# Second products of four experts with tokens as the moving side, their bias in ScalarE's copy and a turn back on TensorE; the last stage's ranks and shares rebuilt; edge codes spread over another loop

## The reference, cut to what matters

```
# first stage: out = prelu(((d_gamma * (q k^T)) v) Wo + bo)      q, k, v = x W + b, 1024 tokens, batch 4
# last stage, on y = layernorm(h):
hg = (y @ W_gat).reshape(M, 4, 4)                    # heads x experts
a_src, a_dst = (hg * att_src).sum(-1), (hg * att_dst).sum(-1)
e = leaky_relu(a_src[src] + a_dst[dst])              # 262144 edges and the loops
alpha = softmax of e over the edges of each dst
agg = segment_sum(hg[src] * alpha, dst) + b_gat
scores = layernorm(agg, ln_gamma, ln_beta).reshape(M, 4, 4).mean(1)
w = softmax(top_k(scores, 2))
for ei in range(4):
    hh = gelu(y @ W1[ei] + b1[ei])
    out = out + g[..., None] * (hh @ W2[ei] + b2[ei])   # g: w where ei is among the two, else 0
```

## Time and profile before

| | us |
|---|---|
| median of 3 runs | 1418.79 (1412.3 to 1440.24) |
| the profiled execution's own time | 1412.49 |
| its span in the trace | 1410.0 |

### The profile page before, as it was taken

One profiled execution on the slowest core, in us unless ns is written; L12 is line 12 of the kernel. 1 busy time (PEld: TensorE's weight loads), 2 busy tenths in 40 slices (PEclk: granted clock), 3 DMA queues, 4 the chain that ended last, 5 costly groups with the idle time before them and its releaser, 6 DMA issues. The chain is left out here.

```text
span 1410.0 us, 29905 instructions
## 1 busy us (share of the span) xinstructions
PE 1122.6 (80%) x11867; PEld 648.3 (46%) x11867; DVE 985.3 (70%) x2120; ACT 460.0 (33%) x855; POOL 277.9 (20%) x312
## 2 busy tenths in 40 slices
PE   2499279999999999999938999995956989588440
PEld 1232144556555565555626333333425767577340
DVE  3645547898888889898355355554464994799977
ACT  1120144355534344343325344443111233322120
POOL 0000450010010101001003000000000577777505
PEclk9799689999999999999955899997975696799785
DMA  6000220000000000000010443402020211011001
GB/s 217 0 8 16 81 91 2 3 2 3 2 3 13 7 2 3 3 2 7 10 57 6 106 90 82 87 5 49 20 66 0 17 10 10 9 10 9 0 1 31
DMA packets 54835, 40.15 MB, mean 28 GB/s; under 512 B 27171, under 2 KB 51363, under 8 KB 53684
## 3 DMA queue, kind: packets, MB, share of 16 engines
q1 hardware_dynamic: 49588, 36.70, 10.3%
q0 software_dynamic: 5120, 1.65, 1.6%
HBM read 14.80 MB, written 4.94 MB: 14 GB/s over the span
## 5 line engine op out<-in xcount | busy, mean ns | idle before, releaser
L1100 DVE CUSTOM_DVE_ANT_0 ps<-ps,arena 128x512 f32<-128x512 f32 (+3 forms) x384 | 209.0, 595 | 60.1 <-PE ps L878 59.1
L1046 ACT ACTIVATE arena<-ps 128x512 f32<-128x512 f32 (+1 forms) x320 | 160.0, 552 | 211.3 <-PE ps L903 211.2
L892 PE MATMUL ps<-arena 32*128 32x256 f32 (+3 forms) x1856 | 213.9, 350 | 3.1 <-ACT arena L1046 2.3
L878 PE MATMUL ps<-arena 32*128 32x512 f32 (+3 forms) x768 | 167.4, 531 | 9.9 <-DVE arena L1100 9.4
L892 PEld LDWEIGHTS ps<-arena 32*128 32x128 f32 (+1 forms) x1856 | 138.1, 183 | 73.3 <-issue 49.7
L1865 POOL DMA_INDIRECT arena<-node_table,arena x160 | 151.9, 949 | 55.5 <-issue 48.4
L1450 DVE TENSOR_SCALAR arena<-ps 128x704 bf16<-128x704 f32 x96 | 85.6, 892 | 78.1 <-PE ps L1393 78.1
L817 POOL TENSOR_SCALAR_AFFINE_SELECT arena<-arena 128x512 f32<-128x512 f32 (+1 forms) x72 | 41.5, 597 | 459.9 <-ACT arena L1046 413.2
L925 PE MATMUL ps<-arena 128*32 128x256 f32 (+3 forms) x1856 | 110.3, 322 | 0.9 <-POOL arena L817 0.3
L929 PE MATMUL ps<-arena 128*32 128x256 f32 (+3 forms) x1856 | 106.3, 312 | 0.0
L1430 ACT ACTIVATE arena<-ps 128x704 bf16<-128x704 f32 x96 | 72.2, 757 | 97.1 <-PE ps L1393 97.1
(11 more groups left out here) (299 smaller groups left out, 1848.8 us busy)
## 6 DMA issues: line engine op xcount, KB each, us to landing
arena<-arena SPq DMA_DIRECT2D x144, 88.0 KB, 2.2
arena<-in_L_tok_d_gamma_batched SPq DMA_DIRECT2D x4, 1024.0 KB, 13.6
arena<-node_table,arena POOLq DMA_INDIRECT x160, 2.4
arena<-xT SPq DMA_DIRECT2D x8, 264.0 KB, 4.1
xT<-in_L_ffn_edge_index SPq DMA_DIRECT2D x2, 1024.0 KB, 7.6
dT<-arena SPq DMA_DIRECT2D x12, 88.0 KB, 2.1
arena<-in_x SPq DMA_DIRECT2D x4, 256.0 KB, 9.4
dT<-arena SPq DMA_DIRECT2D x8, 128.0 KB, 2.3
```

The lines of the kernel that those rows point to most:

```text
L878: last = pe.matmul(to[:, hd % 2, at:at + wd], qu[r, P * j:P * j + P], ku[r, lo:lo + wd], start=(at == 0), stop=True, skip_group_check=True)
L892: pe.matmul(to[0:r, hd % 2, at:at + wd], ku[d, P * j:P * j + r], qu[d, lo:lo + wd], start=(at == 0), stop=False, skip_group_check=True)
L1046: last = act.activation(to[:, x, 0:at + wd], src[:, x, 0:at + wd], ACT.Exp, scale=unit)
L1100: last = dve.tensor_tensor_reduce(tile, tile, distance[:, first:first + wd], 1.0, most if lo > 0 else -3e38, ALU.add, ALU.max, most)
```

## The change

1. **Edge codes.** The 16 instructions become 32 on half the columns. They are issued between VectorE's products with gamma, from the third step (g = 2) up to g = 26 of the 32, by `while g >= 2 and edges < min(32, 32*(g-1)//25)`. `shi` and `dhi` lie in `keys` and `tmp` now. The loads of the edge list are issued after those of gamma and of the second pair.
2. **The row of ones** is set once, by GpSimd, in the second norm; VectorE's two memsets go.
3. **Features** use 64 rows of `xT` and `wg`, so nothing waits for a zeroed row; the expert products wait until the features are copied out of PSUM banks 0 and 1.
4. **Second products**: `W2` of an expert is stationary (64 wide), the 384 tokens of hidden values move; two experts fill the two halves of a PSUM bank. ScalarE copies that bank with the bias `b2` as a per-partition operand, TensorE turns the result back with 3 transposes, and ScalarE copies the turned chunk as before. There are four hidden tiles instead of two, and the second half of a chunk is worked off in the next one, so that there are 12 rounds for 11 chunks. GpSimd's addition of `b2` goes.
5. **Last stage**: no scaling of the mean and of the average (folded into other constants), gamma's product placed behind the variance, rank constants set by GpSimd, comparisons by distance (3 instructions for each of 3 distances, over 99, 66 and 33 columns). The shares of experts 0 and 1 are applied by VectorE, those of 2 and 3 by ScalarE in 66 instructions of 64 columns; VectorE adds all four, in three thirds of 11 tiles, each written out by its own DMA. GpSimd takes no part.

```diff
-            chain(dve.tensor_scalar(near, src, float(N - 1), None, ALU.is_lt))
...
-            chain(dve.tensor_tensor(far, far, tmp, ALU.add))
-            assert n == EDGE_STEPS, n
...
+                    while g >= 2 and edges < min(EDGE_STEPS, EDGE_STEPS * (g - 1) // (EDGE_END - 2)):
+                        edge(edges)
+                        edges += 1
...
-            if r < 2:
-                dve.memset(xT[D:D + 1, :], 1.0)
...
+    def ones_row(pool):
+        pool.memset(m["xT"][D:D + 1, :], 1.0)
...
-        pe.wait_ge(self.loaded, 112)
-        pe.wait_ge(self.step, 1)
+        pe.wait_ge(self.loaded, 96)
...
-            flat = outE.rearrange("p (k c) -> p k c", k=NT)
-            pool.wait_ge(tables.expd, 2)
-            pool.tensor_tensor(flat, flat, b2.rearrange("p (o c) -> p o c", o=1).broadcast_to([P, NT, FE * D]), ALU.add)
...
+            pe.wait_ge(tables.step, 2)
+            for i in range(NXC + 1):
                 products(pe, i)
                 if i < NB:
                     count(i)
             pe.wait_ge(zeroed, 1)
-            pe.wait_ge(tables.step, 3)
+            pe.wait_ge(kept, NXC)
...
+        def project(c, p):
+            pe.wait_ge(gel, FE * c + 2 * p + 2)
+            if c > 0:
+                pe.wait_ge(biased, 2 * (c - 1) + p + 1)
+            for x in range(2):
+                e = 2 * p + x
+                last = pe.matmul(ps[D * x:D * x + D, 4 + p, 0:CW], w2[:, D * e:D * e + D], hh[e], start=True, stop=True)
+            last.then_inc(projected, 1)
...
+        def turn_back(c, p):
+            pe.wait_ge(biased, 2 * c + p + 1)
+            if c > 0:
+                pe.wait_ge(kept, c)
             for t in range(3):
+                last = pe.transpose(ps[:, t // 2, 256 * (t % 2) + P * p:256 * (t % 2) + P * p + P], y[p][:, P * t:P * t + P], ident[:])
+            last.then_inc(back, 1)
+        if i < NXC:
+            hidden(0)
+            hidden(1)
+        if i > 0:
+            project(i - 1, 1)
+            turn_back(i - 1, 0)
+        if i < NXC:
+            hidden(2)
+            hidden(3)
+            project(i, 0)
+        if i > 0:
+            turn_back(i - 1, 1)
...
+            act.activation(y[p], ps[:, 4 + p, 0:CW], ACT.Identity, bias=b2[p]).then_inc(biased, 1)
...
+            for r in range(3):
+                for e in (2, 3):
+                    for k in range(THIRD * r, THIRD * r + THIRD):
+                        last = act.activation(o4[:, k, e, :], o4[:, k, e, :], ACT.Identity, scale=ex[:, k, e:e + 1])
+                    last.then_inc(shared, 1)
...
+            for apart in range(1, FE):
+                c = FE - apart
+                chain(dve.tensor_tensor(first[:, :, 0:c], sc[:, :, 0:c], sc[:, :, apart:], ALU.is_ge))
+                chain(dve.tensor_tensor(rank[:, :, apart:], rank[:, :, apart:], first[:, :, 0:c], ALU.add))
+                chain(dve.tensor_tensor(rank[:, :, 0:c], rank[:, :, 0:c], first[:, :, 0:c], ALU.subtract))
...
+            for r in range(3):
+                tiles = slice(THIRD * r, THIRD * r + THIRD)
+                for e in range(FE):
+                    if e < 2:
+                        share = ex[:, tiles, e:e + 1].broadcast_to([P, THIRD, D])
+                        chain(dve.tensor_tensor(o4[:, tiles, e, :], o4[:, tiles, e, :], share, ALU.mult))
+                    else:
+                        dve.wait_ge(shared, 2 * r + e - 1)
+                    chain(dve.tensor_tensor(h3[:, tiles, :], h3[:, tiles, :], o4[:, tiles, e, :], ALU.add))
+                dve.sem_inc(fin, 1)
```

More of the change, by code:

```diff
@@ L1764, in graph_experts @@
     kint, klo, srci, dhi, ta, tb, kf, dlob = ends
-    load, products, gelus, credits = expert_chunks(m, outE)
+    load, products, gelus, kept = expert_chunks(m, outE)
     att_s, att_d, bg, gamma, beta = (full.take(P, HE) for _ in range(5))
-    b2, wg = full.take(P, FE * D), full.take(D + 1, HE)
+    wg = full.take(D + 1, HE)
     loaded = sem("f_loaded")
@@ L1920, in add @@
                 last.then_inc(added, 1)
-            for i in range(NXC):
+            pe.wait_ge(tables.step, 2)
+            for i in range(NXC + 1):
                 products(pe, i)
@@ L1955, in _ @@
         def _(act):
-            credits(act)
-            for i in range(NXC):
+            for i in range(NXC + 1):
                 gelus(act, i)
@@ L2439, in combine_experts @@
     o4 = outE.rearrange("p (k e d) -> p k e d", k=NT, e=FE)
-    def combine(eng, chain, tiles):
-        for e in range(FE):
-            share = ex[:, tiles, e:e + 1].broadcast_to([P, tiles.stop - tiles.start, D])
-            chain(eng.tensor_tensor(o4[:, tiles, e, :], o4[:, tiles, e, :], share, ALU.mult))
-            chain(eng.tensor_tensor(h3[:, tiles, :], h3[:, tiles, :], o4[:, tiles, e, :], ALU.add))
     with nc.Block() as block:
@@ L2488, in _ @@
             chain(dve.tensor_reduce(one[1], sq, X, ALU.add))
-            dve.tensor_scalar(one[1], one[1], 1.0 / HE, EPS, ALU.mult, ALU.add).then_inc(pgate, 1)
+            dve.tensor_scalar(one[1], one[1], 1.0 / HE ** 3, EPS, ALU.mult, ALU.add).then_inc(pgate, 1)
+            dve.wait_ge(ready, FE + 1)
+            chain(dve.tensor_tensor(agg, agg, vecs(gamma), ALU.mult))
             dve.wait_ge(pgate, 2)
@@ L2596, in credits, with bias @@
-    def credits(act):
-        act.sem_inc(outm, 1)
-        act.sem_inc(outk, 1)
-    return load, products, gelus, credits
+            if i > 0:
+                act.wait_ge(projected, 2 * (i - 1) + e // 2 + 1)
+            act.activation(hh[e], ps[:, 2 + e % 2, 0:CW], ACT.Gelu).then_inc(gel, 1)
+        def bias(c, p):
+            act.wait_ge(projected, 2 * c + p + 1)
+            if c > 0:
+                act.wait_ge(back, 2 * (c - 1) + p + 1)
+            act.activation(y[p], ps[:, 4 + p, 0:CW], ACT.Identity, bias=b2[p]).then_inc(biased, 1)
@@ new lines, in gelus @@
+        if i == 0:
+            act.wait_ge(w_in, 80)
+        if i < NXC:
+            gelu(0)
+            gelu(1)
+        if i > 0:
+            bias(i - 1, 1)
+        if i < NXC:
+            gelu(2)
+            gelu(3)
+            bias(i, 0)
+        if i > 0:
+            act.wait_ge(back, 2 * i)
+            act.activation(out3[:, 3 * i - 3:3 * i, :],
+                           ps[:, 0:2, :].rearrange("p b (t c) -> p (b t) c", t=2)[:, 0:3, :], ACT.Copy).then_inc(kept, 1)
+    return load, products, gelus, kept
```

183 lines of the change are left out of this document (86 added, 97 removed).

## The result

The changed kernel takes 1340.89 us at the median of four runs (1334.73 to 1346.55), the kernel before 1416.17 in runs beside it: a ratio of 0.948, 95% interval 0.9429 to 0.9532. It is faster by 75 us where 74 were forecast.

The account below looks back on a forecast made before the run. No engine was taken as full; waits stage by stage, mostly between PE and VectorE, set the end. The terms summed to -73.7 us from the profiled 1412.5, giving 1339 us, range 1326 to 1359.

Parts of the forecast that it names:

- Start: First stage: gamma turned on PE from 26.5 us instead of 53.35, without waiting for the edge codes; -26.8 us.
- Loops: First stage's two loops: edge codes hidden in the first pair, VectorE sets the pace in the second; +8 us.
- Norms: First two norms: two memsets leave VectorE's chain; -7.2 us.
- Features: Last of the graph stage's waits before the one-hots: PE starts features 12.67 us earlier; -14.3 us, -11.5 at the other end.
- The product tail: From the last one-hot to the first lookup: 20.7 us against 27.7, at the higher clock; -7.0 us.
- the rival of the low clock: Expert products: PE's clock stays low, the tail grows by 10 us, 1349 to 1352 in all; chance 0.12.
- GpSimd's addition: Lookups: without the addition of `b2`, VectorE's 64-column instruction of 15.82 us takes 0.2; -15.6 us.
- Scores and ranks: Last stage: scalings and memsets gone, gamma's product moved into a gap, ranks with fewer instructions; -3.4 us.
- Shares: Last stage: VectorE and ScalarE share the work, 17.6 us against 22.7; -5.1 us.
- Output: End of the kernel: the last DMA carries 352 KB instead of 736 KB; -2.3 us.
- Slower than before: Expert products: PE and ScalarE in lockstep, 20 us a chunk, 1460 us in all; chance 0.03.

Follow-up runs that it names:

- the five kernels of the table: Kernels with the old second products on chips with long one-hots: two the change otherwise, three the kernel before without GpSimd's addition, with the new last or first stage; 1545.41 to 1636.79 us.
- the combined form: The change plus codes spread to the last step, stores early, PE kept busy in the norms, gamma's scaling on ScalarE; 1328.7 us, ratio 0.9374 to the kernel before.
- its second profile: The change run once more, unaltered, on a chip without the long one-hots; 1338.38 against 1415.46 us for the kernel before, ratio 0.944.

## Why the prediction was right, and where it was not

*Start*: right as worked out; PE's clock was at 1.00 there (26 to 32 us) and gave one microsecond more. *Loops*: the mechanism was right, VectorE full in the second pair; the term was 8 and measured 5.4. Halves with one tensor cost 0.68 where 0.73 were taken, and VectorE had caught up by 117 us. *Norms*: -9.0 for -7.2, the issue gap of 0.93 us ahead of each memset having been left out. *Features*: right, -13.2 between the two ends of -14.3 and -11.5: VectorE still waited 1.42 us, since PE took 12.69 us over them at a mean clock of 0.57.

*The product tail* came out well, -9.4 for -7.0, but partly by luck. Given a clock of 1.00 the sum was right, and the 2.4 us more are mostly two chunks of 5.1 us instead of 6.0. That the clock would be 1.00 the prediction put down to wider instructions, and that didn't hold as a rule: the old form ran at 1.00 too, and the new one had a mean clock of 0.68 in a tail of 26.4 us and of 0.59 in one of 29.1. These two tails are 8.0 and 10.8 us over the 18.3 of the change, so the rival of the low clock, +10 us, had the right price and came true in two of the six profiles of the new form whose chunks were left as they are. What the record shows of the clock is this. It fell only behind a stand of about 2 us for VectorE's tiles. Once it was down and PE full, the new form was back at 1.00 within 9 to 23 us in eight such spells, while the old form stayed down for 2 us once and for 26 us, to the end of its chunks, in the kernel before, and for 47 to 108 us in the five kernels of the table. So wider instructions may well shorten a low spell, as the prediction supposed, but they don't prevent one. Which phase of that the tail meets was left to chance; in two profiled runs of the change it was the good one. At equal clock the new products gain 0.7 us a chunk, which is hidden, and lose 1.1 behind the last count.

*GpSimd's addition*: right in cause, shown by the run without it and by the second place that it struck; 17.8 for 15.6. The lookups without it are 143 us in the kernel before as in the change, so all 17.8 go with it; the 2.2 us beyond the one instruction go with a clock of 0.89 before and 0.94 in both kernels without the addition. *Scores and ranks*: -2.8 for -3.4; that GpSimd's scaling would start 6.9 us late was missed, and on ScalarE it costs VectorE nothing: 15.13 us in the combined form. *Shares*: 17.6 us as forecast; ScalarE's 66 at 0.24 us each, for 0.25, one wait of 0.81 for 0.9. By the Trainium skill, ScalarE: Activation LUTs, section Rules for kernel authors, such an activation costs about 0.3 us and 0.83 ns a column, which is an estimate of 23 us for the 66. The trace disagrees: each lasts 0.333 us but starts 0.24 after the one before, and the 66 take 15.86. *Output*: -3.4 for -2.3, the last third's DMA landing within 3.5 us of VectorE's end.

*Between*: the 4.4 us between the norms, 4.2 of them in the attention stage, and 1.5 of the last norm were no term at all, and no run shows their cause. They stand against the larger norms, tail, addition and output, -7.5 together, and the start and loops, -3.7; that is why the sum of the terms was within 3.3 us of the 77.0 though single ones were off by more than 2. That part is luck.

*Slower than before* by lockstep: no sign; in the tail a half chunk ran in 2.57 us, and until its chunks were done PE waited for ScalarE once, for 0.20 us.

## What to carry to other kernels

An addition on GpSimd beside small VectorE instructions can cost VectorE nearly its whole length, whichever instruction comes then: the 18 us here cost 15 to 18, so count it at full price. Where VectorE is full and PE waits for its tiles, look for PE's stands of about 2 us and the half clock that can follow them, and don't count on a clock that only the profile of one run shows. And look at each barrier for stores that wait in a queue behind something that they don't need.

## What the runs showed of the hardware

- In the chunks the granted clock fell to 0.50 behind ten of 15 stands of 1.7 to 2.3 us and nowhere else. Two that weren't followed by a fall are those of 2.26 us at 1099.03 in the change and of 2.27 us at 1096.58 in its second profile; in both the next one was.
- Once down, with PE full, the clock stayed at 0.50 for 9 to 23 us with the new products. With the old ones it stayed so for 2 and for 26 us in the kernel before, and for 47 to 108 us behind the long one-hots, where the new ones needed 4 to 8.
- Over transposes alone the clock rose from 0.61 to 1.00, and with two fifths of them it stayed at 1.00 for 70 us.
- GpSimd's first arithmetic after 160 gathers started 6.9 us late in the change and 7.9 us in the kernel before, each time behind a MODIFY_POOL_CONFIG; its memsets didn't start late.
- On two of the four chips of the experiments the one-hots took 203 to 222 us longer in every profile, PE getting an instruction every 2.8 us. Whether it is the gathers' traffic that holds the instructions back wasn't settled.
